# Thirteen held tables instead of ten, gathers in groups that wait for the landing of the group in front, and the second gram between the second and third layer

## The chip, the cores and the metric

One core of one Trainium2 chip. The metric is the device time of one execution in microseconds: 511.42 us, the median of three runs of the kernel before (511.13 to 512.32). Lower is better.

## The reference

2048 samples. For each, 26 rows of 128 floats are looked up, one in each of 26 tables; 13 tables have 1000 rows, the others 1250 to 125000. With the dense row that makes 27 feature vectors. All products of two different vectors (351), then the dense row, enter an MLP of 512, 256 and 1 outputs.

```
e = jnp.stack([tbl_0[ids[:, 0]], ..., tbl_25[ids[:, 25]]], axis=1)
combined = jnp.concatenate([dense[:, None, :], e], axis=1)
z = jnp.einsum('bfd,bgd->bfg', combined, combined)[:, iu, ju]
h = jnp.concatenate([z, dense], axis=1)
h = jnp.maximum(h @ W_top1 + b_top1, 0.0)
h = jnp.maximum(h @ W_top2 + b_top2, 0.0)
y = h @ W_top3
```

## The kernel before

The batch is done in eight turns (`s`) of 256 samples, each turn in two tiles (`t`) of 128. Turn 0 and VectorE's last turn are written out; the others are hardware loops on TensorE, ScalarE and VectorE, while SyncE and GpSimd are unrolled.

**Held tables.** `NUM_HOT` of the tables with 1000 rows stay in SBUF, split in a high and a low part (`hot_hi`, `hot_lo`). In turn 0 ScalarE rounds each (`round_hot`) and VectorE subtracts (`rest`, L264). A lookup of 256 samples is a product with a one-hot mask: VectorE makes the mask by comparing the ids, broadcast to all partitions, with row numbers (`compare`, L277), and TensorE multiplies (`hot`, L458), 8 matmuls with the high and 8 with the low part. `SLOTS` mask buffers are used in turn: the mask of feature f waits until feature f − SLOTS is multiplied (`hot_done`).

**Gathered tables.** The others are fetched by GpSimd, one indirect DMA per table and tile (L252), 64 KB each, into `rows`, in `GROUPS` of up to four features (feature 0 is the dense row, loaded by SyncE). TensorE transposes a group (`transposes`, L472), and ScalarE copies it to `feats`. `rows` holds one tile, so the gathers of a group of the next tile wait for the transposes of this one (`wait_rows_free`).

**Gram.** For each sample, TensorE multiplies 26 × 26 features (`grams`, L483, 128 products a tile, each two matmul records). ScalarE copies the first half of the samples, VectorE the second (`copy_gram`, L260), into `gram`, and nine DMAs of SyncE per tile move `gram` into `pairs` (`move_pairs`, L176), with the pairs on partitions. `pairs` is split in `pairs_hi` (ScalarE, `round_pairs`) and `pairs_lo` (VectorE, L286). Before the moves SyncE waits in `wait_gram`.

**MLP.** Layer 1 (`layer1a`, `layer1b`, L496 to L498) is three matmuls per chunk, in halves of two output blocks; layer 2 is L540 and layer 3 L548. Their ReLUs are on ScalarE (L378). The MLP of turn s − 1 is done within turn s.

**The order** within a turn is one list, `STEPS`, which TensorE and ScalarE both follow: tile 0's units (held pairs of tables and gathered groups mixed, `TILE0`), layer 1a, gram 0, then tile 1's groups mixed with layers 1b and 2, layer 3, gram 1. VectorE's order stands in its `turn`, SyncE's and GpSimd's in their loops. Units take three PSUM banks in turn. The outer loop of GpSimd:

```
for s in range(TURNS):
    for t in range(2):
        for g, features in enumerate(GROUPS):
            wait_rows_free(pool, s, t, g)
            for f in features:
                if f > 0:
                    pool.indirect_dma_start(...).then_inc(gathered[t][g], 16)
```

## Time and profile before

| | us |
|---|---|
| median of three runs | 511.42 |
| the profiled execution | 512.17 |
| its span, first to last instruction | 510.4 |
| TensorE busy (matmul) | 360.0 (71%) |
| VectorE busy | 242.9 (48%) |
| ScalarE busy | 153.6 (30%) |
| GpSimd busy | 254.2 (50%) |
| granted TensorE clock, mean | 0.839 |
| HBM read, whole span | 29.97 MB, 59 GB/s with the writes |

Busy time is a mean over stages. "Issue" is time in which an engine waited for nothing that the profile shows; "remote", or "another core or an unknown queue", is a wait whose releaser the profile cannot name (this kernel has one core). A matmul's end is modelled, its start is recorded. Gathers are the records of GpSimd; a record ends when the descriptors are made, and the data land later.

### The profile page before, as it was taken

The page shows a single profiled execution, that of the slowest core. Times are in us where ns is not written, and L with a number is a line of the kernel's source. Part 1 is how long each engine was busy: PE and PEld are TensorE (multiplying, and loading weights), DVE is VectorE, ACT ScalarE, POOL GpSimd, SP SyncE. Part 2 cuts the span into 40 slices and gives each one's busy share as a digit, 9 for nine tenths or more (in the row PEclk, how much of TensorE's full clock was granted, in tenths as well). Part 3 has the DMA queues.
Part 4 walks back from the last instruction along what each step waited for, and adds up shares of the span by engine and source line. Part 5 has one row for each costly group of instructions (what it writes and reads, how often), then busy time and mean ns, then how long its engine had stood idle before and what let it go on. Part 6 is the DMA issues. An engine that isn't in the chain of part 4 may idle for free.

```text
span 510.4 us, 13987 instructions
## 1 busy us (share of the span) xinstructions
PE 360.0 (71%) x6224; PEld 332.2 (65%) x6224; DVE 242.9 (48%) x172; ACT 153.6 (30%) x269; POOL 254.2 (50%) x260
## 2 busy tenths in 40 slices
PE   7695516977279763989369782897459882798927
PEld 6583406966179762989259781896439881797826
DVE  4995703827048270745429370673509451380220
ACT  2462401234122331324132241233232341223512
POOL 5887560655506474265635755264734745165000
PEclk9988656999569995899759986898959986698978
DMA  7992230211202131121303112131312112111000
GB/s 198 251 278 54 55 90 7 79 43 51 78 17 80 36 87 46 34 65 39 94 26 77 46 45 79 29 74 31 102 31 66 47 41 84 26 54 41 16 15 1
DMA packets 23322, 33.32 MB, mean 65 GB/s; under 512 B 6565, under 2 KB 15397, under 8 KB 23303
## 3 DMA queue, kind: packets, MB, share of 16 engines
q0 software_dynamic: 8192, 16.79, 12.6%
q1 hardware_dynamic: 14926, 16.20, 11.8%
q8 instruction: 12, 0.20, 0.2%
q10 hardware_dynamic: 186, 0.09, 0.1%
q14 instruction: 6, 0.05, 0.0%
HBM read 29.97 MB, written 0.01 MB: 59 GB/s over the span
## 4 chain that ended last, share of the span: by engine, by line
PE 56%; issue 18%; another core or an unknown queue 14%; ACT 7%; DMA 3%; SPq 2%; DVE 1%; ACTq 0%; DVEq 0%
PE psum L458 31%; PE psum L483 11%; PE psum L472 3%; DMA lows<-table 3%; ACT feats L336 3%; PE psum L548 3%; PE psum L496 2%; PE psum L497 2%; PE psum L498 2%; ACT gram L336 2%; PE psum L540 1%; ACT h L378 1%; SPq L208 1%; ACT dense_hi L336 1%
## 5 line engine op out<-in xcount | busy, mean ns | idle before, releaser
L252 POOL DMA_INDIRECT rows<-table,idx x256 | 254.0, 992 | 215.0 <-PE psum L472 114.2
L277 DVE TENSOR_TENSOR onehot<-ids_b,psum 125x2048 fp32r<-125x2048 int16 x80 | 180.2, 2283 | 18.5 <-PE psum L458 12.3
L260 DVE COPY gram<-psum 26x416 f32<-26x416 f32 x64 | 37.4, 584 | 182.6 <-PE psum L483 181.1
L336 ACT ACTIVATE feats<-psum 128x512 f32<-128x512 f32 (+1 forms) x120 | 77.4, 689 | 148.1 <-PE psum L458 106.9
L458 PE MATMUL psum<-onehot,hot_hi 125*128 125x256 f32 x640 | 99.2, 299 | 11.1 <-issue 6.8
L483 PE MATMUL psum<-feats 128*26 128x26 f32 x4096 | 64.3, 211 | 59.6 <-issue 55.7
L483 PEld LDWEIGHTS psum<-feats 128*26 128x26 f32 x4096 | 55.9, 125 | 70.8 <-issue 64.8
L458 PE MATMUL psum<-onehot,hot_lo 125*128 125x256 f32 x640 | 95.6, 291 | 4.4 <-issue 4.3
L458 PEld LDWEIGHTS psum<-onehot,hot_hi 125*128 125x128 f32 x640 | 86.5, 200 | 14.2 <-issue 9.0
L458 PEld LDWEIGHTS psum<-onehot,hot_lo 125*128 125x128 f32 x640 | 86.7, 198 | 6.3 <-issue 5.6
L336 ACT ACTIVATE gram<-psum 26x416 f32<-26x416 f32 (+1 forms) x72 | 35.5, 494 | 73.1 <-PE psum L483 54.5
L548 PE MATMUL psum<-h,w_sb 128*1 128x256 f32 x32 | 13.2, 560 | 60.2 <-ACT h L378 60.2
L378 ACT ACTIVATE h<-psum,b_sb 128x256 f32<-128x256 f32 x44 | 18.4, 470 | 102.2 <-remote 78.4
L548 PEld LDWEIGHTS psum<-h,w_sb 128*1 128x1 f32 x32 | 2.5, 99 | 66.4 <-ACT h L378 62.2
L472 PE MATMUL psum<-ident_sb,rows 128*128 128x128 f32 x272 | 42.0, 282 | 0.0
L496 PE MATMUL psum<-pairs_hi,w_hi 126*128 126x256 f32 (+1 forms) x96 | 28.5, 297 | 9.0 <-DVE pairs_lo L286 9.0
L472 PEld LDWEIGHTS psum<-ident_sb,rows 128*128 128x128 f32 x272 | 32.9, 145 | 1.2
L540 PE MATMUL psum<-h,w_sb 128*128 128x256 f32 x128 | 29.0, 379 | 0.0
L286 DVE TENSOR_TENSOR pairs_lo<-pairs,pairs_hi 126x768 fp32r<-126x768 f32 x8 | 7.9, 987 | 43.3 <-ACT pairs_hi L336 34.3
L497 PE MATMUL psum<-pairs_lo,w_hi 126*128 126x256 f32 (+1 forms) x96 | 28.2, 294 | 0.0
L498 PE MATMUL psum<-pairs_hi,w_lo 126*128 126x256 f32 (+1 forms) x96 | 28.1, 293 | 0.0
L540 PEld LDWEIGHTS psum<-h,w_sb 128*128 128x128 f32 x128 | 23.7, 190 | 2.9
(26 smaller groups left out, 167.7 us busy)
## 6 DMA issues: line engine op xcount, KB each, us to landing
lows<-table SPq DMA_DIRECT2D x10, 448.0 KB
rows<-table,idx POOLq DMA_INDIRECT x256, 2.5
ids_b<-hot_ids SPq DMA_DIRECT2D x8, 384.0 KB
ids_b<-hot_ids SPq DMA_DIRECT2D x8, 256.0 KB
rows<-dense SPq DMA_DIRECT2D x16, 64.0 KB
lows<-w SPq DMA_DIRECT2D x1, 1024.0 KB
pairs<-gram SPq DMA_DIRECT2D x16, 39.0 KB
lows<-table SPq DMA_DIRECT2D x10, 52.0 KB
```

The costliest lines, as they stand in the source:

```text
L252: pool.indirect_dma_start(out=rows[:, f, :], out_offset=None, in_=tables[f - 1], in_offset=bass.IndirectOffsetOnAxis(ap=idx[:, 2 * s + t, ...
L260: return nc.vector.tensor_copy(o, x)
L277: nc.vector.tensor_tensor(onehot[f % SLOTS][0:HP_ROWS, :, :], ids_b[0:HP_ROWS, f:f + 1, :].to_broadcast([HP_ROWS, HC, SB]), psum[0:HP_ROWS ...
L336: return nc.scalar.activation(o, x, ACT.Copy)
L458: mm = nc.tensor.matmul(psum[:, bank, (f % 2) * SB:(f % 2 + 1) * SB], part[0:HP_ROWS, f, c, :], onehot[f % SLOTS][0:HP_ROWS, c, :], start= ...
L472: mm = nc.tensor.transpose(psum[:, bank, m * P:(m + 1) * P], rows[:, f, :], ident_sb[:, :])
L483: mm = nc.tensor.matmul(psum[32 * q:32 * q + NJ, GP[h], k * NJ:(k + 1) * NJ], feats[:, t, n, 0:NJ], feats[:, t, n, 1:NF], start=True, stop ...
L496: nc.tensor.matmul(o, w_hi, x_hi, start=(n == 0), stop=False)
L497: nc.tensor.matmul(o, w_hi, x_lo, start=False, stop=False)
L498: return nc.tensor.matmul(o, w_lo, x_hi, start=False, stop=(n == ZC))
L540: mm = nc.tensor.matmul(psum[:, HP[0], m * SB:(m + 1) * SB], w2_sb[:, c, m * P:(m + 1) * P], h1[:, c, :], start=(c == 0), stop=(c == C1 - 1))
L548: mm = nc.tensor.matmul(psum[0:1, HP[1], 0:SB], w3_sb[:, m:m + 1], h2[:, m, :], start=(m == 0), stop=(m == C2 - 1))
```

## The change

- `NUM_HOT` goes from 10 to 13: the gathered tables go from 16 to 13, the groups from five (3, 4, 4, 4 and 1 gathers) to four (3, 4, 4 and 2), the held pairs from five to seven (the last has one table).
- `SLOTS` goes from 4 to 3. VectorE makes three masks ahead, and the `compare` in front of the second `copy_gram` is gone. `AHEAD` (4) keeps the rounding of tables in turn 0 as it was. The first part of the ids, loaded in two DMAs, is now three features, the second ten.
- `TILE0` has a new order. Layer 2 stands behind all of tile 1's transposes, gram 1 behind layer 2, layer 3 behind gram 1.
- GpSimd's `wait_landed`: a group's first gather waits until the group in front has landed, across tiles and turns. The third group of tile 0 also waits until the second gram of the turn before is done.
- `pairs_lo` is the memory of `pairs`, read as the other type: VectorE's subtraction overwrites `pairs`. So SyncE's moves of tile 0 wait for layer 1b of the turn before (`mlp_b`) instead of the split.
- The 32 transposes at the start are gone.

```diff
-NUM_HOT = 10
+NUM_HOT = 13
...
-    WARM = 32
...
-    SLOTS = 4
+    SLOTS = 3
+    AHEAD = 4
...
-    TILE0 = [("hot", 0), ("rows", 0, 0), ("hot", 1), ("rows", 0, 1), ("hot", 2), ("rows", 0, 2), ("hot", 3),
-             ("rows", 0, 3), ("hot", 4), ("rows", 0, 4)]
+    TILE0 = [("hot", 0), ("hot", 1), ("rows", 0, 0), ("hot", 2), ("rows", 0, 1), ("rows", 0, 2), ("hot", 3),
+             ("rows", 0, 3), ("hot", 4), ("hot", 5), ("hot", 6)]
...
-             + [("layer", "1b")] + TILE1[1:2] + [("dense",)] + TILE1[2:3] + [("layer", "2")] + TILE1[3:]
-             + [("layer", "3"), ("gram", 1)])
+             + [("layer", "1b")] + TILE1[1:3] + [("dense",)] + TILE1[3:] + [("layer", "2"), ("gram", 1), ("layer", "3")])
...
         pairs = sb("pairs", [P, ZC, SB])
+        pairs_lo = pairs[:, :, :].bitcast(fp32r)
         pairs_hi = sb("pairs_hi", [P, ZC, SB], fp32r)
-        pairs_lo = sb("pairs_lo", [P, ZC, SB], fp32r)
...
             def wait_gram(s, t):
                 if s == 0 and t == 0:
                     sp.wait_ge(zeroed, 1)
-                elif s > 0:
-                    sp.wait_ge(pairs_split, s)
+                elif t == 0:
+
+                    sp.wait_ge(mlp_b, 2 * s - 1)
...
         def _(pool):
+            def wait_landed(s, t, g):
+
+                if g > 0:
+                    t0, g0, s0 = t, g - 1, s
+                else:
+                    t0, g0, s0 = 1 - t, NG - 1, s - (t == 0)
+                if s0 >= 0:
+                    pool.wait_ge(gathered[t0][g0], 16 * sum(f > 0 for f in GROUPS[g0]) * (s0 + 1))
+
...
                         wait_rows_free(pool, s, t, g)
+                        wait_landed(s, t, g)
+                        if s > 0 and t == 0 and g == 2:
+
+                            pool.wait_ge(gram_done[1], 2 * s)
...
                 rest_of_dense(s)
-                if not last:
-                    compare(s + 1, 3, False)
                 copy_gram(dve, copy, 1, s, 1, first)
...
-                            for f in (2 * n[0] + SLOTS, 2 * n[0] + SLOTS + 1):
+                            for f in (2 * n[0] + AHEAD, 2 * n[0] + AHEAD + 1):
...
-            for f in range(SLOTS):
+            for f in range(AHEAD):
                 round_hot(f)
...
-                wait_feats(pe, s, "rows", t, NG - 1)
+                wait_feats(pe, s, *(TILE0, TILE1)[t][-1])
...
-
             pe.wait_ge(ident_in, 16)
-            for n in range(WARM):
-                nc.tensor.transpose(psum[:, HP[0], 0:P], ident_sb[:, :], ident_sb[:, :])
```

TensorE in the loop body, from tile 1's third group to the end of the turn. Before (L472 transposes, L540 layer 2, L548 layer 3, L483 gram):

```order
L472 MATMUL psum<-ident_sb,rows 128x128 [waits feats_out,gathered1_2]
...
L540 MATMUL psum<-h1,w2_sb 128x256 [waits relu_out]
...
L540 MATMUL psum<-h1,w2_sb 128x256 x4
L447 REGISTER_ALU [waits gathered1_3]
L472 MATMUL psum<-ident_sb,rows 128x128 [waits feats_out]
...
L447 REGISTER_ALU [waits gathered1_4]
L472 MATMUL psum<-ident_sb,rows 128x128 [waits feats_out]
L546 REGISTER_ALU
L548 MATMUL psum<-h1,w3_sb 1x256 [waits relu_out]
...
L483 MATMUL psum<-feats 26x26 [waits gram_out0]
```

The same piece now (L484 transposes, L552 layer 2, L495 gram, L560 layer 3):

```order
L484 MATMUL psum<-ident_sb,rows 128x128 [waits feats_out,gathered1_2]
...
L459 REGISTER_ALU [waits gathered1_3]
L484 MATMUL psum<-ident_sb,rows 128x128 [waits feats_out]
...
L552 MATMUL psum<-h,w_sb 128x256 [waits relu_out]
...
L552 MATMUL psum<-h,w_sb 128x256 x4
...
L495 MATMUL psum<-feats 26x26 [waits gram_out0]
...
L495 MATMUL psum<-feats 26x26 [waits gram_out1]
...
L560 MATMUL psum<-h,w_sb 1x256 [waits relu_out]
```

The transposes have moved in front of layer 2, and the gram stands between layer 2 and layer 3.

GpSimd's gathers from the start, before:

```order
L252 DMA rows<-table,idx 128x128 [waits idx_in]
L252 DMA rows<-table,idx 128x128 x15
L252 DMA rows<-table,idx 128x128 [waits rows_done]
L252 DMA rows<-table,idx 128x128 x2
L252 DMA rows<-table,idx 128x128 [waits rows_done]
L252 DMA rows<-table,idx 128x128 x3
```

And now, the second turn's groups 1 to 3 of tile 0:

```order
L266 DMA rows<-table,idx 128x128 [waits gathered0_0,rows_done]
L266 DMA rows<-table,idx 128x128 x3
L266 DMA rows<-table,idx 128x128 [waits gram_done1,gathered0_1,rows_done]
L266 DMA rows<-table,idx 128x128 x3
L266 DMA rows<-table,idx 128x128 [waits gathered0_2,rows_done]
L266 DMA rows<-table,idx 128x128
```

Every group has gained a wait for `gathered` of the group in front, and one group in eight a wait for `gram_done1`.

## Rows read from the trace of the kernel before

**Rows 1.** The page, the chain that ended last, by engine
```profile
PE 56%; issue 18%; another core or an unknown queue 14%; ACT 7%; DMA 3%; SPq 2%; DVE 1%; ACTq 0%; DVEq 0%
```

**Rows 2.** Windows: us, busy PE, PEld, DVE, ACT, POOL (instructions), clock, DMA share, GB/s
```profile
83.50:146.50 63.00, 44.14 (x774) 40.50 (x774) 28.82 (x21) 17.48 (x32) 30.48 (x32) 0.83 0.20 54
...
265.30:323.95 58.65, 42.46 (x775) 39.64 (x775) 28.61 (x21) 17.57 (x33) 31.24 (x32) 0.85 0.22 56
...
440.60:510.40 69.80, 54.87 (x842) 50.78 (x842) 22.84 (x21) 21.52 (x41) 15.09 (x16) 0.88 0.10 24
```

**Rows 3.** TensorE in turn 4: start, us, instructions [idle before, releaser]
```profile
284.44 1.12 PE L458 MATMUL psum<-onehot,hot_hi 125*128 125x256 f32 x8
285.40 1.12 PE L458 MATMUL psum<-onehot,hot_lo 125*128 125x256 f32 x8
...
290.57 0.44 PE L483 MATMUL psum<-feats 128*26 128x26 f32 x10 [1.06 <-issue]
...
293.63 2.95 PE L483 MATMUL psum<-feats 128*26 128x26 f32 x241 [1.19 <-issue]
296.52 0.65 PE L472 MATMUL psum<-ident_sb,rows 128*128 128x128 f32 x4
...
300.76 3.62 PE L540 MATMUL psum<-h,w_sb 128*128 128x256 f32 x16
304.22 0.71 PE L472 MATMUL psum<-ident_sb,rows 128*128 128x128 f32 x5
314.77 1.44 PE L548 MATMUL psum<-h,w_sb 128*1 128x256 f32 x3 [9.84 <-ACT h L378]
```

**Rows 4.** GpSimd in turn 4, its gathers
```profile
291.40 0.94 POOL L252 DMA_INDIRECT rows<-table,idx  x1 [0.30 <-issue]
297.44 0.94 POOL L252 DMA_INDIRECT rows<-table,idx  x1 [5.10 <-PE psum L472]
...
310.25 0.95 POOL L252 DMA_INDIRECT rows<-table,idx  x1 [0.30 <-issue]
314.18 0.94 POOL L252 DMA_INDIRECT rows<-table,idx  x1 [2.98 <-remote]
```

**Rows 5.** ScalarE in turn 4, the ReLUs of layers 1a and 2
```profile
293.79 0.84 ACT L378 ACTIVATE h<-psum,b_sb 128x256 f32<-128x256 f32 x2 [3.35 <-remote]
...
313.88 0.84 ACT L378 ACTIVATE h<-psum,b_sb 128x256 f32<-128x256 f32 x2 [9.68 <-remote]
```

**Rows 6.** TensorE in turn 7, layer 3 and the second gram
```profile
481.50 1.02 PE L548 MATMUL psum<-h,w_sb 128*1 128x256 f32 x4 [0.38 <-ACT h L378]
482.43 2.56 PE L483 MATMUL psum<-feats 128*26 128x26 f32 x256
```

**Rows 7.** The gathers' line, its duration and time from issue to landing
```profile
L252 POOL DMA_INDIRECT rows<-table,idx x256: 938/944/2111, 3.6 to 468.4; - x128
...
DMA to landing us min/median/max: 2.5/2.5/4.4
```

**Rows 8.** VectorE in turn 0, the masks of the last two tables
```profile
34.51 2.29 DVE L277 TENSOR_TENSOR onehot<-ids_b,psum 125x2048 fp32r<-125x2048 int16 x1
...
37.84 2.29 DVE L277 TENSOR_TENSOR onehot<-ids_b,psum 125x2048 fp32r<-125x2048 int16 x1
```

**Rows 9.** Turn 0: TensorE's grams, and GpSimd's first and last gather between them
```profile
45.47 0.57 PE L483 MATMUL psum<-feats 128*26 128x26 f32 x45 [2.82 <-ACT feats L336]
...
55.68 0.94 POOL L252 DMA_INDIRECT rows<-table,idx  x1 [3.69 <-PE psum L472]
...
58.98 0.55 PE L483 MATMUL psum<-feats 128*26 128x26 f32 x42 [1.12 <-ACT feats L336]
...
74.41 0.94 POOL L252 DMA_INDIRECT rows<-table,idx  x1 [0.30 <-issue]
...
78.71 2.34 PE L483 MATMUL psum<-feats 128*26 128x26 f32 x179 [0.50 <-issue]
```

**Rows 10.** SyncE in turn 4, the transfers of a tile's pairs
```profile
299.18 7.24 SPq L176 DMA_DIRECT2D pairs<-gram  x9
```

More of the change, by code:

```diff
@@ L43, in dlrm_tower @@
     HOT = [list(range(f, min(f + 2, NH))) for f in range(0, NH, 2)]
-    assert NG == 5 and len(HOT) == 5 and C1 == 4 and C2 == 2
-    TILE0 = [("hot", 0), ("rows", 0, 0), ("hot", 1), ("rows", 0, 1), ("hot", 2), ("rows", 0, 2), ("hot", 3),
-             ("rows", 0, 3), ("hot", 4), ("rows", 0, 4)]
+    assert NG == 4 and len(HOT) == 7 and C1 == 4 and C2 == 2
+    TILE0 = [("hot", 0), ("hot", 1), ("rows", 0, 0), ("hot", 2), ("rows", 0, 1), ("rows", 0, 2), ("hot", 3),
+             ("rows", 0, 3), ("hot", 4), ("hot", 5), ("hot", 6)]
     TILE1 = [("rows", 1, g) for g in range(NG)]
```

## The prediction

> **What bounds the kernel now.** I read the chain of waits first, then the turns by windows, then one turn engine by engine, then the first and the last turn.
>
> The chain [rows 1] is TensorE for 56%. It also holds 18% "issue" and 14% released by nobody the profile knows. So VectorE (48% busy) isn't the bound, and neither is the bandwidth. The turns [rows 2] show the shape: the kernel runs eight. From 83.5 to 440.6 us six equal ones take 357.1 us, 59.5 each, with TensorE busy for 42 to 44. Some 16 us of each turn are TensorE standing still.
>
> Where they stand is in turn 4, TensorE [rows 3]. From 265.3 to 286.5 it works without a gap on the held tables. After layer 1a the first gram begins at 290.57 and issues 10 matmuls. It then drips, and its other 241 come in one piece of 2.95 us at 293.63. Layer 2 and the last transposes end by 304.9. Layer 3 begins at 314.77, after 9.84 us of waiting for ScalarE. The second gram drips again and ends near 323.9.
>
> ScalarE [rows 5] waited for layer 2's signal until 313.88, although the last layer 2 matmul was over by 304.4. GpSimd [rows 4] issues a gather per 1.25 us (0.95 and 0.30 idle) without a pause from 297.44 to 311.2 and goes on at 314.18. At the first gram it is the same: the last gather ends at 292.34, the gram flows at 293.63, and layer 1a's signal reaches ScalarE at 293.79, over 4 us after its end. The control is turn 7 [rows 6], where no gathers are left: layer 3 waits 0.38 us, and all 256 matmuls of a gram take 2.56. The worst case is turn 0 [rows 9]: the second gram begins at 58.98, and 179 of its matmuls come in a piece at 78.71, after a run of gathers up to 75.35. **Reading:** while gathers run back to back, TensorE's completion signals come late, and tiny matmuls soon stop; both clear about 1.5 to 3 us after the last gather. That is inferred from coincidence, five places of one trace.
>
> The Trainium skill says the opposite (SBUF — State Buffer, "SBUF: two separate sides"): engine ports and DMA ports are disjoint, and a DMA and a compute operation cannot slow each other. By it the pauses buy nothing; that is the second rival below. Rows 3 to 6 speak against it here.
>
> **The change, part by part.**
>
> *More held tables.* Three tables move from gathers to one-hot matmuls. One table is 16 matmuls per turn, two pieces of 0.96 us [rows 3]: 1.91 us. Three are 5.7, less three transposes of 0.1: the table phase goes from 21.3 to 26.7 us on TensorE. VectorE must make 13 masks per turn at 2.29 us [rows 8]. Only three are made ahead now (onehot has three buffers, not four), so ten follow inside the phase: 22.9, behind the first feature (1.9) and perhaps 1 us of late signal, and ahead of the last feature (1.9): 27.7. VectorE passes TensorE by a little. I take 28.0. VectorE's whole turn, 13 masks (29.8) and the 5.7 that turn 4's 28.6 hold besides ten masks [rows 2], is 35.5 and doesn't bound.
>
> *Fewer and paced gathers.* 26 per turn instead of 32, in eight groups. A gather takes 2.5 us from issue to landing, 4.4 at most [rows 7]. With 1.25 us from gather to gather [rows 4] a pause costs 2.5 − 1.25, and some 0.2 for the wait: 1.5 us. GpSimd then needs 26 × 1.25 + 8 × 1.5 = 44.5 us per turn, under the turn I arrive at, so not a bound. At 4.4 us to landing it would be 57.7.
>
> *First gram.* Groups 2 and 3 of the first tile start once gram 1 is done, a little before the table phase, and land some 10 us into it. Tile 1's thirteen gathers and four pauses follow: 16.3 + 6 = 22.3, landed at 32.3. Gram 0 could start at 28.0 + 3.0 for layer 1a, so it drips for 1.3 us and ends at 35.3. Layer 1a is 286.5 to 289.5, where the 1.06 us of idle time before the gram's first piece begin [rows 3]; with the gram it was 9.9 us to 296.5, now 7.3.
>
> *Middle.* First transposes, layer 1b, transposes, layer 2: 296.5 to 304.9, 8.4 us; three transposes fewer, 8.1.
>
> *Second gram before layer 3.* Today 304.9 to 323.95, 19.05 us. Only groups 0 and 1 of the next first tile may now run before the gram is done: 3 × 1.25 + 1.5 and 4 × 1.25 + 1.5, 11.8 us from the first transposes at 35.5, so landed at 47.3. The gram stands ready at 43.4, drips, and ends at 47.3 + 2.6 = 49.9; ScalarE's ReLU of layer 2 is hidden under it; layer 3 adds 1.2, between the 1.0 and 1.4 of its records [rows 3, 6]: 51.1. This part is 7.7. Bounds: 4 from turn 7 [rows 6], where nothing drips, and 19 if nothing is cured.
>
> *Pairs in place.* pairs_lo now overwrites pairs, so the transfers of tile 0's pairs wait for layer 1b, 3.5 us behind gram 0, instead of a split long past. SyncE issues nine in 7.2 us [rows 10] and then the ids, for ten tables instead of six. They would start some 39 us into the turn, all be issued at 46, landed at 48.5. The copies of gram 1 want them at 49.9. Covered by 1.4 us; without that cover every late us delays VectorE's fourth mask.
>
> Sum of a turn: 28.0 + 7.3 + 8.1 + 7.7 = 51.1. Six turns: 306.6 against 357.1, **−50.5**.
>
> *Turn 0.* VectorE paces it: a mask and a split every 3.33 us [rows 8], three more, +10. The three more tables to load (1.5 MB) hide behind that pace. Gram 0 drips from 45.47 to 54.4 today [rows 9]; the gathers have landed before the later start, −5. Gram 1 took 24.4 us; now two groups and the gram, 14.4, −10. Together **−5**. The 32 transposes at the start vanish: at 1.2 instead of 2.4 GHz a feature takes at most twice its 1.91 us, 3.8, against a pace of 3.33, so 0.5 us each for a few features. I cost that at nothing, at most 2 us.
>
> *Turn 7.* Its table phase took 25.7 (a stall of 3 in it), now 28.0; a first gram perhaps 1.3 longer, layer 3 1.0 out of the way: **+2.6**.
>
> Total −52.9. The profiled execution took 512.17 us (span 510.4 and 1.8 around it); that gives 459.3. The median shown is 0.75 below it: **458.5 us**.
>
> **The rivals.**
>
> 1. *Gathers cost nothing any more.* If groups of at most four leave no backlog, both grams run as in turn 7: a turn is 27.5 + 6.3 + 8.1 + 4.0 = 45.9, six save 81.7 of 357.1 instead of 50.5, the time is 427. For: the table phases of turns 4 to 6 run beside groups of three and four gathers without a gap on TensorE; those of turns 1, 2 and 7 have a gap of 3 us, each beside eight gathers in a row. Against: a gram issues far faster than the tables' matmuls, and the one of turn 0 stopped 3.3 us after the gathers began anew, so within one group.
>
> 2. *The gathers were not the cause.* Then the late signal (9.9) and both drips stay: the turn is 28 + 9.8 + 8.1, 9.9 of waiting with half a gram under it, and 4.5 for the rest and layer 3: 60.3. Six turns cost 5, turn 0 10, turn 7 2: 528. Turn 7 and the instants of release speak against it. This is what the rule of the Trainium skill's SBUF page would do here.
>
> 3. *Late signals meet three mask buffers, and it is slower.* A buffer's round is a mask 2.29, a feature 1.91 and the signal's lateness L, over three buffers. At L = 1 the round is 1.7 per feature, hidden; from L = 2.7 it passes VectorE's 2.29. At 4.3, as after layer 1a [rows 3, 5], it is 2.83 per feature and the phase 36.8. With 23.1 for the rest a turn is 59.9, six cost 2, turn 0 saves 5 as before, turn 7 costs 11: 520. It decides from L = 4, a phase of 35.6. For: the lateness is seen. Against: the table phase at 284.44 runs on beside gathers, and TensorE waits for no mask there.
>
> 4. *Landing becomes the bound.* At 4.4 us to landing GpSimd needs 57.7 per turn: 6 × 57.7 = 346, the time is 498. Against: 4.4 is the worst, and the median 2.5 holds beside the pairs' transfers.
>
> The Trainium skill (DMA: Bandwidth & Descriptors, "Anatomy of one DMA") puts a gather's fixed cost at about 2.0 us, most of it the receipt of the write. By its figure, as an estimate, GpSimd needs 26 × 1.25 + 8 × 2.0 = 48.5 us per turn, still under the turn; the trace's median, 2.5 to landing, is of that size.
>
> **How the numbers follow.** My forecast, with its sizes off by up to 3 us per turn either way, has 0.72. Rival 1 has 0.13, rival 4 0.08, rival 2 0.03, rival 3 0.03, and 0.01 is for a wash. Three us on six turns and 5 on the first give 436 to 481; reaching toward rivals 1 and 4, the range is 430 to 486. About 0.2% is what a measurement of this kernel tells from no change. Faster 0.93, same 0.01, slower 0.06.
>
> **What would show it.** GpSimd's gathers stand in groups of two to four, with pauses near 1.5 us that a landing ends. ScalarE's wait for layer 2 falls from 10 us to under 4. Second grams end within 3 us of group 1's landing. Turns last 49 to 54 us, turn 0 some 78 to its end, and VectorE is busy for about 300 us. I am wrong if the wait before layer 3 stays near 10, if the table phase shows gaps of TensorE for VectorE's masks (over 30 us), or if GpSimd never waits for anything but landings.

## The result, and the profile after

The changed kernel takes **483.8 us** (median of 4, 477.34 to 485.17) against 511.87 us for the kernel before (4 runs, 511.13 to 512.34): ratio 0.9411, 95% interval 0.9318 to 0.9503. It is faster, as forecast, but by 28 us and not by 53: inside the range of 430 to 486, near its upper end. The four runs spread by 1.6%, where the kernel before spreads by 0.2%. The profiled execution took 484.05 us. The lines here are the page's: the busy time of each engine, TensorE's granted clock in 40 slices, and the chain by engine.

```profile
span 482.2 us, 14732 instructions
...
PE 393.7 (82%) x6528; PEld 361.2 (75%) x6528; DVE 298.3 (62%) x199; ACT 159.8 (33%) x272; POOL 204.5 (42%) x212
...
PEclk9975975799889999899989998999979998999968
...
PE 70%; issue 11%; DMA 10%; POOL 4%; SPq 2%; DVE 1%; ACT 1%; POOLq 0%; ACTq 0%
```

TensorE is 70% of the chain where it was 56% [rows 1]. "Issue" fell from 18% to 11%, and the 14% whose releaser the profile can't name are gone. Three stretches, the second and third answering to [rows 2] (window, its length, busy time and instructions of PE, PEld, DVE, ACT and POOL, clock, DMA share, GB/s):

```profile
87.50:142.40 54.90, 49.17 (x823) 45.98 (x817) 36.14 (x25) 17.54 (x31) 24.91 (x27) 0.91 0.22 59
248.40:301.90 53.50, 48.05 (x817) 43.13 (x816) 35.68 (x25) 17.92 (x32) 25.52 (x27) 0.97 0.20 57
408.90:482.20 73.30, 60.09 (x885) 54.87 (x884) 30.79 (x24) 22.00 (x41) 17.79 (x19) 0.93 0.10 26
```

Turns 1 to 6 begin at 87.5, 142.4, 196.1, 248.4, 301.9 and 356.0, turn 7 at 408.9: six in 321.4 us, 53.6 each, where 51.1 was predicted. Turn 0 ends at 87.5 (predicted 78.5), and what follows 408.9 lasts 73.3 (predicted 72.4). TensorE in turn 4, after the table phase of 248.4 to 276.3 (start, length, instruction, count, idle before it and what ended it):

```profile
279.26 0.67 PE L495 MATMUL psum<-feats 128*26 128x26 f32 x40
280.39 2.05 PE L495 MATMUL psum<-feats 128*26 128x26 f32 x216 [0.46 <-issue]
282.40 0.65 PE L484 MATMUL psum<-ident_sb,rows 128*128 128x128 f32 x4
...
290.62 0.52 PE L495 MATMUL psum<-feats 128*26 128x26 f32 x39
291.99 2.03 PE L495 MATMUL psum<-feats 128*26 128x26 f32 x145 [0.86 <-issue]
294.48 0.25 PE L495 MATMUL psum<-feats 128*26 128x26 f32 x5 [0.47 <-issue]
...
298.83 0.18 PE L495 MATMUL psum<-feats 128*26 128x26 f32 x1 [0.45 <-issue]
299.55 0.76 PE L495 MATMUL psum<-feats 128*26 128x26 f32 x45 [0.53 <-issue]
...
300.48 1.49 PE L560 MATMUL psum<-h,w_sb 128*1 128x256 f32 x3
```

The first gram flows almost at once (before: 10 matmuls, then a drip [rows 3]). The second begins at 290.62, flows for 184 matmuls, drips from 294.48 to 299, and ends in a piece of 45. Layer 3 follows without a wait. Turn 4 is shown because the kernel before was read there, and it isn't typical: of the six turns it has the shortest first gram and the longest second one. In turn 2 the second gram drips at its start instead, and is done sooner:

```profile
188.19 0.50 PE L495 MATMUL psum<-feats 128*26 128x26 f32 x36
...
192.08 2.38 PE L495 MATMUL psum<-feats 128*26 128x26 f32 x214 [0.53 <-issue]
```

In turn 4 ScalarE's ReLU of layer 2 waits 1.88 us instead of 9.68 [rows 5]:

```profile
290.72 0.84 ACT L390 ACTIVATE h<-psum,b_sb 128x256 f32<-128x256 f32 x2 [1.88 <-issue]
```

GpSimd's gathers in the same turn, the first of a group each but for 297.61, which is the last of its group (the idle time in brackets is the pause; within a group it is 0.30):

```profile
248.31 0.94 POOL L266 DMA_INDIRECT rows<-table,idx  x1 [4.45 <-DMA rows<-table,idx]
...
267.68 0.94 POOL L266 DMA_INDIRECT rows<-table,idx  x1 [2.32 <-DMA rows<-table,idx]
...
274.68 1.26 POOL L266 DMA_INDIRECT rows<-table,idx  x1 [2.31 <-DMA rows<-table,idx]
...
293.87 0.94 POOL L266 DMA_INDIRECT rows<-table,idx  x1 [2.99 <-DMA rows<-table,idx]
...
297.61 0.95 POOL L266 DMA_INDIRECT rows<-table,idx  x1 [0.31 <-issue]
301.14 0.94 POOL L266 DMA_INDIRECT rows<-table,idx  x1 [2.59 <-PE psum L495]
```

The gram flows again 1.0 us after the last gather has ended (297.61 + 0.95, then 299.55), and the gram's end releases the next gather at 301.14. From 248.31 to 301.14 are 52.8 us for 26 gathers and eight pauses, as long as the turn. It isn't GpSimd's time alone: three of the eight pauses end by TensorE, two by its transposes and one by the gram. In four of the six turns the wait for the gram is 4.5 to 4.8 us long, as here in turn 2, up to 2.5 longer than the shortest wait for a landing (2.3):

```profile
195.28 0.94 POOL L266 DMA_INDIRECT rows<-table,idx  x1 [4.79 <-PE psum L495]
```

So the two engines wait for each other by turns. Turn 0, first GpSimd and then TensorE:

```profile
14.12 1.79 POOL L266 DMA_INDIRECT rows<-table,idx  x1 [7.10 <-DMA rows<-table,idx]
...
27.82 0.94 POOL L266 DMA_INDIRECT rows<-table,idx  x1 [7.33 <-DMA rows<-table,idx]
...
40.97 0.94 POOL L266 DMA_INDIRECT rows<-table,idx  x1 [7.67 <-DMA rows<-table,idx]
```

```profile
40.75 1.11 PE L484 MATMUL psum<-ident_sb,rows 128*128 128x128 f32 x4 [9.90 <-DMA rows<-table,idx]
```

A group's pause is over 7 us there, beside the load of the held tables, and TensorE waits 9.90 us for rows.

### The profile page after: what moved, and what is told of

Its sections match the earlier page's. It is cut to its first block, busy times and chain, and to the rows that moved or that the text cites. A ratio compares the mean times of both kernels' runs of the same rounds, so it can differ in the third digit from the quotient of the medians.

```text
span 482.2 us, 14732 instructions
## 1 busy us (share of the span) xinstructions
PE 393.7 (82%) x6528; PEld 361.2 (75%) x6528; DVE 298.3 (62%) x199; ACT 159.8 (33%) x272; POOL 204.5 (42%) x212
## 3 DMA queue, kind: packets, MB, share of 16 engines
q0 software_dynamic: 6656, 13.64, 10.8%
## 4 chain that ended last, share of the span: by engine, by line
PE 70%; issue 11%; DMA 10%; POOL 4%; SPq 2%; DVE 1%; ACT 1%; POOLq 0%; ACTq 0%
PE psum L470 37%; PE psum L495 11%; DMA rows<-table,idx 8%; PE psum L552 5%; PE psum L484 5%; POOL rows L266 4%; PE psum L508 4%; PE psum L509 3%; PE psum L510 3%; SPq L176 2%; PE psum L560 2%; DMA pairs<-gram 1%; DVE gram L274 0%; DVE onehot L291 0%; DMA idx<-ids 0%
## 5 line engine op out<-in xcount | busy, mean ns | idle before, releaser
L266 POOL DMA_INDIRECT rows<-table,idx x208 | 204.3, 982 | 238.8 <-DMA rows<-table,idx 125.6
L291 DVE TENSOR_TENSOR onehot<-ids_b,psum 125x2048 fp32r<-125x2048 int16 x104 | 232.1, 2283 | 35.2 <-PE psum L470 25.2
L470 PE MATMUL psum<-onehot,hot_hi 125*128 125x256 f32 x832 | 125.8, 295 | 16.2 <-ACT hot_hi L348 10.6
L470 PEld LDWEIGHTS psum<-onehot,hot_hi 125*128 125x128 f32 x832 | 110.4, 197 | 25.9 <-issue 18.6
L470 PE MATMUL psum<-onehot,hot_lo 125*128 125x256 f32 x832 | 118.4, 286 | 0.0
L470 PEld LDWEIGHTS psum<-onehot,hot_lo 125*128 125x128 f32 x832 | 108.6, 194 | 0.6
L495 PE MATMUL psum<-feats 128*26 128x26 f32 x4096 | 61.8, 202 | 45.0 <-issue 43.5
L495 PEld LDWEIGHTS psum<-feats 128*26 128x26 f32 x4096 | 51.3, 115 | 57.5 <-issue 54.0
L484 PE MATMUL psum<-ident_sb,rows 128*128 128x128 f32 x224 | 34.2, 287 | 16.2 <-DMA rows<-table,idx 16.2
L484 PEld LDWEIGHTS psum<-ident_sb,rows 128*128 128x128 f32 x224 | 26.5, 147 | 17.6 <-DMA rows<-table,idx 16.9
L390 ACT ACTIVATE h<-psum,b_sb 128x256 f32<-128x256 f32 x44 | 18.4, 470 | 47.2 <-PE psum L510 24.7
L509 PE MATMUL psum<-pairs,w_hi 126*128 126x256 f32 (+1 forms) x96 | 29.0, 302 | 0.0
L552 PE MATMUL psum<-h,w_sb 128*128 128x256 f32 x128 | 28.9, 379 | 0.0
L552 PEld LDWEIGHTS psum<-h,w_sb 128*128 128x128 f32 x128 | 23.6, 190 | 2.9
L508 PEld LDWEIGHTS psum<-pairs_hi,w_hi 126*128 126x128 f32 (+1 forms) x96 | 20.3, 211 | 5.5 <-DVE pairs L300 5.5
L509 PEld LDWEIGHTS psum<-pairs,w_hi 126*128 126x128 f32 (+1 forms) x96 | 20.3, 212 | 0.0
L510 PEld LDWEIGHTS psum<-pairs_hi,w_lo 126*128 126x128 f32 (+1 forms) x96 | 20.1, 210 | 0.0
```

The costliest lines, as they stand in the source:

```text
L266: pool.indirect_dma_start(out=rows[:, f, :], out_offset=None, in_=tables[f - 1], in_offset=bass.IndirectOffsetOnAxis(ap=idx[:, 2 * s + t, ...
L291: nc.vector.tensor_tensor(onehot[f % SLOTS][0:HP_ROWS, :, :], ids_b[0:HP_ROWS, f:f + 1, :].to_broadcast([HP_ROWS, HC, SB]), psum[0:HP_ROWS ...
L390: nc.scalar.activation(dst[:, c, :], psum[:, bank, n * SB:(n + 1) * SB], ACT.Relu, bias=bias[:, c:c + 1]).then_inc(relu_out, 1)
L470: mm = nc.tensor.matmul(psum[:, bank, (f % 2) * SB:(f % 2 + 1) * SB], part[0:HP_ROWS, f, c, :], onehot[f % SLOTS][0:HP_ROWS, c, :], start= ...
L484: mm = nc.tensor.transpose(psum[:, bank, m * P:(m + 1) * P], rows[:, f, :], ident_sb[:, :])
L495: mm = nc.tensor.matmul(psum[32 * q:32 * q + NJ, GP[h], k * NJ:(k + 1) * NJ], feats[:, t, n, 0:NJ], feats[:, t, n, 1:NF], start=True, stop ...
```

## The experiments

Each kernel ran with the kernel before beside it. Kernels 1 to 8 (the first two sets) ran on one chip, where the kernel before took 511.63 and 513.67 us; the result's own runs, with 511.87, are counted with it. **Kernels 9 to 11 came onto a second chip of the same kind and kernel 12 onto a third, where the kernel before took 384.17 and 384.06 us**, at a granted clock of 0.96 instead of 0.84. Times are compared only within a chip; kernel 12 stands beside the other three because the kernel before takes the same on both. Kernels 2, 3, 4, 9 and 12 leave out lookups, so they give times and no usable result. Diffs are cut where `...` stands.

| kernel | us | ratio to before, 95% | turn, us |
|---|---|---|---|
| **first chip** | | | |
| before | 511.6 / 513.7 | 1 | 59.5 |
| changed (the result above) | 483.8 | 0.941 [0.932, 0.950] | 53.6 |
| 1. no pauses, no gate | 556.75 | 1.086 [1.080, 1.093] | 65.5 |
| 2. no gathers after turn 0 | 421.1 (one run) | | 44.9 |
| 3. plain loads by GpSimd | 418.29 (one run) | | 46.1 |
| 4. plain loads by SyncE | 413.85 (one run) | | 45.5 |
| 5. pauses alone on the kernel before | 548.52 | 1.068 [1.060, 1.076] | 61.8 |
| 6. no gate | 487.44 | 0.952 [0.945, 0.959] | 54.7 |
| 7. free start | 471.73 | 0.919 [0.913, 0.926] | 53.7 |
| 8. gate one group earlier | 494.23 | 0.966 [0.958, 0.974] | 54.6 |
| **second chip** | | | |
| before | 384.17 | 1 | |
| 9. rows in order, no pauses, no gate | 427.36 | 1.113 [1.107, 1.119] | 47.7 |
| 10. free start, up to two groups | 414.91 | 1.079 [1.076, 1.083] | 46.2 |
| 11. free start, pauses at the grams | 423.76 | 1.103 [1.101, 1.106] | 47.3 |
| **third chip** | | | |
| before | 384.06 | 1 | |
| 12. changed, rows in order | 461.07 | 1.201 [1.192, 1.211] | 51.8 |

A turn is the mean of turns 1 to 6 of the one profiled execution, from the start of one table phase to the next.

**1. No pauses, no gate.** Does the gain come from pausing, or from tables and order?

```diff
-                        wait_landed(s, t, g)
-                        if s > 0 and t == 0 and g == 2:
-                            pool.wait_ge(gram_done[1], 2 * s)
```

> The changed kernel with thirteen held tables, without the wait for landings and without the wait for the second gram: gathers run back to back as rows come free. Theory A (back-to-back gathers hold up TensorE's signals and its small matmuls): runs of seven or more gathers return, and with them waits of 8 us and more after layer 2 and grams of over 8 us; 500 to 530 us. Rival B (the pauses buy nothing; the gain comes from three tables fewer to gather and from the order): 470 to 485 us.

Measured 556.75 us, beyond both ranges. The pauses and the gate are worth 73 us; thirteen tables and the new order without them are 45 us slower than the kernel before. TensorE, then GpSimd's first and last of 13 gathers in a row, then two groups of the waits of the whole run (engine, line, releaser: us in all, times, longest):

```profile
266.91 0.36 PE L491 MATMUL psum<-feats 128*26 128x26 f32 x18
268.49 0.23 PE L491 MATMUL psum<-feats 128*26 128x26 f32 x3 [1.23 <-issue]
...
278.59 2.81 PE L491 MATMUL psum<-feats 128*26 128x26 f32 x221 [1.13 <-issue]
```

```profile
259.84 0.95 POOL L262 DMA_INDIRECT rows<-table,idx  x1 [16.29 <-PE psum L480]
...
275.09 0.94 POOL L262 DMA_INDIRECT rows<-table,idx  x1 [0.30 <-issue]
```

```profile
ACT h L386 <- remote: 55.2, 5, 11.5
...
DVE onehot L287 <- remote: 43.0, 8, 6.3
```

The gram begins at 266.91, stops 0.4 us later, and issues one to three matmuls at a time until the gathers end at 276.03; the rest comes in one piece 2.6 us later. "Remote" is a signal without a sender that the profile knows: VectorE's masks wait 43 us for such ones, and the table phase takes 35.6 us instead of 28. That is part of rival 3, whose own figure for the phase was 36.8. But not each signal is late, as it assumed: VectorE waits 6.3 us for one, and at the same time the table matmuls, 256 columns wide, stop like the small ones. In the same turn, from the tenth gather since 226.53 on:

```profile
239.88 0.52 PE L466 MATMUL psum<-onehot,hot_hi 125*128 125x256 f32 x3
...
243.41 0.28 PE L466 MATMUL psum<-onehot,hot_hi 125*128 125x256 f32 x1 [1.12 <-issue]
...
247.93 2.07 PE L466 MATMUL psum<-onehot,hot_hi 125*128 125x256 f32 x8 [1.17 <-DVE onehot L287]
```

A table that takes 1.9 us elsewhere takes from 239.88 to 246.8. The mask for the next one ends the wait last, 1.17 us later; the two delays lie over each other. So the reading "tiny matmuls stop" was too narrow.

**2. No gathers after turn 0.**

```diff
-                            if f > 0:
+                            if f > 0 and s == 0:
...
```

The pauses, and TensorE's waits for rows, go after turn 0 too.

> The changed kernel, but tables are gathered in turn 0 alone; later turns use the rows that lie there, so seven eighths of the lookups of the thirteen gathered tables are left out. Theory A: grams of 2.6 to 3.1 us, no wait of over 1 us for layer 2's signal, turns of 46 us, 425 to 435 us in all. Rival C (the drip is TensorE's own, from a low clock or from its instruction stream): grams still drip and the turns stay over 51 us, 465 to 480.

421.1 us, 4 below theory A's range, with grams (2.3 us) and turns (44.9) a little below those it named. Rival C is out. So the gathers still cost the changed kernel 63 us on this chip, of which turns 1 to 6 hold 52 (6 × 8.7).

**3. Plain loads in place of the gathers.** GpSimd issues them, with no pause and no gate; each moves 128 consecutive rows. The page counts 6656 packets and 13.64 MB in GpSimd's queue in either kernel.

```diff
-                            if f > 0:
+                            if f > 0 and s > 0:
+                                pool.dma_start(rows[:, f, :], tables[f - 1][P * (s % 7):P * (s % 7) + P, :]).then_inc(gathered[t][g], 16)
+                            elif f > 0:
```

> As the kernel without pauses, but from turn 1 on each indirect gather is a plain load of 128 consecutive rows of the same table, issued by GpSimd: the lookups of turns 1 to 7 are left out, the number and size of the transfers is the same. If what holds up TensorE is GpSimd making descriptors, or packets landing in SBUF, the time is that of the kernel without pauses within 3%, with the same drips. If it is the indirection itself, it comes near the kernel without gathers (425 to 440).

418.29 us, below the figure of the second theory (425 to 440) and far from the first. The rows are GpSimd's, then TensorE's:

```profile
248.81 5.27 POOL L262 DMA_DIRECT2D rows<-table  x10 [1.71 <-PE psum L482]
```

```profile
252.56 3.43 PE L493 MATMUL psum<-feats 128*26 128x26 f32 x256
255.81 1.02 PE L558 MATMUL psum<-h,w_sb 128*1 128x256 f32 x4
```

Ten loads in a row, 0.53 us each, run until 254.1, into a gram of which all 256 matmuls come in one piece, with layer 3 right behind. The same bytes, in as many packets, from the same queue, into the same place hold up next to nothing (this gram takes 3.3 us instead of 2.3). Traffic into SBUF as such is not what delays TensorE on this chip; the indirect gather is, by its form, the reading of its indices, its longer time on GpSimd (0.94 us against 0.53), or its scattered rows.

**4. The same loads from SyncE.** Against kernel 3, with the matching waits on TensorE:

```diff
+            def load_rows(s, t):
+                for g, features in enumerate(GROUPS):
+                    wait_rows_free(sp, s, t, g)
+                    for f in features:
+                        if f > 0:
+                            sp.dma_start(rows[:, f, :], tables[f - 1][P * (s % 7):P * (s % 7) + P, :]).then_inc(
+                                plain_in[t][g], 16)
...
```

> The same plain loads, issued by SyncE instead of GpSimd, without pauses; the lookups of turns 1 to 7 are left out. Theory A1 (it is GpSimd's making of descriptors in software, not the traffic): grams of 2.6 to 3.1 us, turns of 46 to 48 us, 430 to 450 in all. Theory A2 (it is packets that land in SBUF): grams and signals as late as with GpSimd's loads, within 4% of that kernel.

413.85 us, 4.4 less: what it costs that GpSimd issues them is small (one run each). It lies below A1's range, and within A2's 4%, which says nothing now that neither kernel has late grams. SyncE's queue moves the same 11.9 MB in 26208 packets where GpSimd's took 5824, so many small packets don't hold up TensorE either: a gram still takes 2.3 us.

**5. Pauses alone, on the kernel before.** Ten tables, old order, four mask buffers.

```diff
...
                         wait_rows_free(pool, s, t, g)
+                        wait_landed(s, t, g)
```

> The kernel before with one part of the change alone: a group of gathers begins when the one in front has landed. Ten held tables, the old order and four mask buffers stay. Theory (gathers in a row hold up small matmuls and TensorE's signals, whatever the order): the waits of about 10 us ahead of layer 2 and the drip of the first gram go, two to four us a turn less for each; but 17 gathers per tile with pauses of 2 to 4 us fill more of GpSimd's time. 485 to 500 us. Rival (the gain of the pauses comes only with the new order, since the old one has other things to fill the late signals): 505 to 515 us. A third way: with 34 gathers a turn and the pauses GpSimd becomes the bound, 515 us or more.

548.52 us, 35 *slower* than before; the third way. A turn of it:

```profile
342.90:405.20 62.30, 48.00 (x774) 43.77 (x774) 28.51 (x21) 17.39 (x32) 30.61 (x32) 0.83 0.19 53
```

GpSimd has 32 gathers a turn (not the 34 of the expectation) and ten pauses of 2.3 to 3.2 us: 32 × 1.25 and 10 × 2.2 make 62, and the turn is 62.3. So pauses alone don't pay with this many gathers. The parts of the change do not add up: pauses alone +35, tables and order alone +45, together −28.

**6. No gate.**

```diff
-                        if s > 0 and t == 0 and g == 2:
-                            pool.wait_ge(gram_done[1], 2 * s)
```

> The changed kernel without the one extra wait of GpSimd on the second gram; the wait for landing stays. Theory (gathers beside a gram cost it time): the second gram of each turn gets more gathers beside it and takes 1 to 3 us more, 484 to 505 us. Rival (the pauses are enough, and the extra wait only costs GpSimd time, which is nearly full): 470 to 480 us.

487.44 us against 483.8. It lies in the theory's range, but with overlapping intervals (0.952 and 0.941): a gain of the gate of some 4 us is likely and not established. In the profiled execution the second gram and layer 3 take 10.5 us a turn instead of 8.9, as the theory has it, and the first gram 0.8 less.

**7. Free start.** In turn 0 the first tile's gathers wait for nothing.

```diff
-                        wait_landed(s, t, g)
+                        if s > 0 or t == 1:
+                            wait_landed(s, t, g)
```

> The changed kernel, where the gathers of the first tile of turn 0 wait for nothing. Theory (in turn 0 the gathers land late because each pause waits for packets that share the queues with the tables' load, 7 to 8 us a pause; TensorE waits 9.9 us for one): 8 to 9 us less, all of it in turn 0, about 475 us. Rival (gathers in a row hold up the table phase of turn 0 just as much): no gain, 480 to 486 us.

**471.73 us, 12 less than the change**, and turn 0 ends at 75.1 instead of 87.5, all of the difference; a turn is 53.7 as before. The theory's 8 to 9 us were too few. (How much of the 12.4 is the edit is known only roughly: kernels 6 and 8 start turn 0 like the changed one and end it at 86.0 and 80.3.) GpSimd still has two long pauses there, but TensorE waits only 0.3 us for rows in turn 0:

```profile
28.39 0.95 POOL L267 DMA_INDIRECT rows<-table,idx  x1 [7.18 <-DMA rows<-table,idx]
...
40.50 0.94 POOL L267 DMA_INDIRECT rows<-table,idx  x1 [8.67 <-DMA rows<-table,idx]
```

It is the best real version on the first chip.

**8. Gate one group earlier.**

```diff
-                        if s > 0 and t == 0 and g == 2:
+                        if s > 0 and t == 0 and g == 1:
```

> The changed kernel, where GpSimd's extra wait on the second gram stands one group earlier, so that no group of the next turn but the first is gathered beside it. Theory (the gram's 11 us instead of 7.7 are the gathers beside it): it takes 3 to 6 us less per turn, 450 to 465 us. Rival (GpSimd then has too little time left for its groups, and the wait moves to the transposes of the rows): 484 us or more.

494.23 us, 10 more: the rival, on the time. In the profiled execution, its fastest (488.78), the turns are 1.0 us longer. The theory was right about the part that it named: the second gram and layer 3 take 4.3 us instead of 8.9, nearly the 3.9 of the kernel without gathers. But the gathers held back there come later: layer 1a and the first gram take 11.9 instead of 8.7, the table phase 29.3 instead of 27.6, the middle 0.7 more. The gathers' cost is moved, not saved.

**9. Rows in order, no pauses, no gate** (kernel 1 with other indices).

```diff
-        "ids": by_tile(ids)[:, :, cold].transpose(1, 0, 2),
+        "ids": np.broadcast_to(np.arange(128, dtype=np.int32)[:, None, None],
+                               (128, batch // 128, len(cold))),
```

> The changed kernel without pauses and without the gate (556.75 us), where the same indirect gathers read the rows 0 to 127 of each table in order instead of the looked up ones (it leaves out the lookups of the thirteen or so tables that are not held). It tells apart what the plain loads of the same 13.64 MB left open (418.29 us without any pause). Theory A (the form of the gather itself holds up the signals: one descriptor for each of 128 indices that the gather has to read first): about as slow, 530 to 557 us. Theory B (rows scattered over HBM do it): 415 to 440 us.

427.36 us, inside range B, and yet it proves nothing of B: it ran on the second chip, where the kernel before takes 384. There a gram beside an unbroken row of gathers looks like this (TensorE, then two of GpSimd's gathers, which stand every 1.25 us from 249.61 to 261.12):

```profile
255.44 0.76 PE L491 MATMUL psum<-feats 128*26 128x26 f32 x66
256.55 4.98 PE L491 MATMUL psum<-feats 128*26 128x26 f32 x190 [0.35 <-issue]
261.38 1.02 PE L556 MATMUL psum<-h,w_sb 128*1 128x256 f32 x4
```

```profile
253.35 0.94 POOL L262 DMA_INDIRECT rows<-table,idx  x1 [0.30 <-issue]
...
259.87 0.94 POOL L262 DMA_INDIRECT rows<-table,idx  x1 [0.30 <-issue]
```

It slows to 26 ns a matmul in its second piece, where a gram with nothing beside it takes 9, but it flows after one stop of 0.35 us, and layer 3 starts at once. So gathers still cost a gram something here: this one takes 5.9 us instead of 2.4. Rows in order aren't the reason why it is so little: kernel 11 shows the same with looked up rows.

**10. Free start, up to two groups under way.** With looked up rows again; a group waits for the one two in front.

```diff
-                if g > 0:
-                    t0, g0, s0 = t, g - 1, s
-                else:
-                    t0, g0, s0 = 1 - t, NG - 1, s - (t == 0)
+                n = NG * (2 * s + t) + g - 2
+                s0, t0, g0 = n // (2 * NG), n // NG % 2, n % NG
```

> The changed kernel with the gathers of the first tile free (471.73 us), where a group waits for the landing of the group two in front of it instead of the one in front, so up to eight gathers are under way. Theory (what harms is how many gathers stand in a row, and GpSimd's 50 us a turn are no bound of the turn): between the unpaced 556.75 and 471.73, 480 to 510 us. Rival (GpSimd's pauses are by now what a turn waits for): 455 to 470 us.

414.91 us, a comparison across chips and so neither. A turn of it:

```profile
212.60:257.10 44.50, 44.18 (x817) 41.89 (x816) 34.87 (x24) 17.84 (x33) 24.80 (x26) 1.00 0.25 68
```

44.5 us with TensorE busy for 44.2 and a clock of 1.00: this is nearly the turn that the kernel without gathers had on the first chip (43.8 to 44.4 in its turns 2 to 6), here with real gathers. It is also 12.5 us faster than kernel 9, which never waits: there the second gram and layer 3 take 6.5 to 7.8 us in turns 2 to 6, here 4.7. Kernel 10 has the gate and up to two groups under way, kernel 9 neither, and other indices; which of these gains the 12 us was not tried.

**11. Free start, pauses only at the grams.** Four of a turn's eight groups pause.

```diff
-                        if s > 0 or t == 1:
+                        if (s > 0 and t == 0 and g < 2) or (t == 1 and g > 1):
```

> The changed kernel with the gathers of the first tile free (471.73 us), and pauses only ahead of the four groups of a turn that stand beside the small matmuls of the grams and transposes; the four that fall in the table phase follow one another without a pause. Theory (only matmuls of a few columns and the handing over between engines suffer): the table phase stays at 28 us and GpSimd gains 6 to 12 us a turn, 455 to 472 us. Rival (gathers in a row hold up the table phase too, whose masks wait for TensorE's signals): its 28 us become 31 or more, 485 to 520 us.

423.76 us, 9 more than kernel 10; the range was made for the first chip. A second gram, beside a group of four looked up gathers that start at 254.87:

```profile
256.13 3.11 PE L496 MATMUL psum<-feats 128*26 128x26 f32 x120
259.65 1.39 PE L496 MATMUL psum<-feats 128*26 128x26 f32 x136 [0.41 <-issue]
```

Beside such a group the changed kernel's gram on the first chip issued one to six matmuls at a time; here it goes on at 26 ns each. The second gram and layer 3 take 5.7 to 6.9 us in turns 2 to 6 instead of 4.7: the pauses put gathers off until they run beside the gram. So between kernels 10 and 11 more pausing costs time, and between kernels 9 and 10 some restraint gains it.

**12. The change whole, rows in order.** Kernel 9's edit of the indices, made to the changed kernel; pauses and gate in place.

> The changed kernel whole, pauses and gate in place, where the gathers read the rows 0 to 127 of each table in order (it leaves out the lookups of the tables that are not held). What it tells depends on the chip, which the time of the kernel before shows. Where that is about 512 us, as in the first two sets of runs: theory A (the form of the gather holds up the signals, wherever its rows lie) 478 to 490 us, theory B (rows scattered over memory do it) 420 to 445 us. Where it is about 384 us, as in the third set: nothing is held up there, so A and B give the same, and the pauses only cost time: 425 to 445 us, 10 to 16 per cent slower than the kernel before; if pausing costs nothing there, 412 to 424 us.

It fell on the third chip, where the kernel before takes 384: 461.07 us, beyond the range given, and 34 more than kernel 9, which differs in pauses and gate alone (and in the chip). The waits show where (GpSimd's for landings, TensorE's transposes for rows):

```profile
POOL rows L266 <- DMA rows<-table,idx: 124.7, 45, 7.4
...
PE psum L484 <- DMA rows<-table,idx: 38.4, 13, 9.2
```

TensorE now waits for rows that the paced GpSimd brings late: 51.8 us a turn against 47.7.

## Why the prediction was right in sign and 25 us off

Part by part, in its own steps. The parts of a turn in us, mean of turns 1 to 6 of one profiled execution each (of turns 2 to 6 where none is paused), from the starts of TensorE's records:

| part | forecast | changed (shortest, longest) | no gate | gate earlier | no pauses | no gathers |
|---|---|---|---|---|---|---|
| table phase | 28.0 | 27.6 (27.3, 28.0) | 27.9 | 29.3 | 35.6 | 27.0 |
| layer 1a, first gram | 7.3 | 8.7 (6.1, 9.8) | 7.8 | 11.9 | 5.3 | 5.3 |
| middle | 8.1 | 8.5 (8.0, 9.5) | 8.5 | 9.2 | 8.0 | 8.0 |
| second gram, layer 3 | 7.7 | 8.9 (7.7, 11.3) | 10.5 | 4.3 | 16.0 | 3.9 |
| turn | 51.1 | 53.6 | 54.7 | 54.6 | 64.9 | 44.2 |

- **Table phase 28.0:** 27.3 to 28.0. Right, also that three mask buffers would do once the signals are no longer late; experiment 1 shows 35.6 when they are. (TensorE's "21.3 to 26.7" doesn't add up: 5.6 more than 21.3 is 26.9. Nothing hangs on it.)
- **First gram 7.3, middle 8.1, second gram and layer 3 7.7:** too short by 1.4, 0.4 and 1.2. In turn 4 alone it looks otherwise, 6.1, 8.2 and 11.3.
- **A pause costs 1.5 us:** the mis-sized term of the turn. Against the usual 0.30 the pauses cost 2.0 at best and up to 4.2 beside other transfers. In turns 1 to 6 the 31 waits that a landing ended hold 82.1 us, 2.65 each, so 2.35 more than the usual. By that, as an estimate, GpSimd needs 26 × 1.25 + 8 × 2.35 = 51.3 us without ever waiting for TensorE, and not 44.5. The 6.6 us of slack I had left it are gone, and "not a bound" was wrong. I took the landing time's median where the wait is for the last of a group, and counted no other transfers beside it. Experiment 5 shows a turn that is GpSimd's round, and experiment 8 that GpSimd can't make up a later start.
- **How it surfaces:** the gathers land later than forecast, the grams drip until they do, the second gram's end opens the gate, and the gathers behind it hold up the next first gram. This closed round of two engines is argued from the rows and from the parts of kernels 6 and 8, not tried by itself. Six turns: 321.4 instead of 306.6, +14.8.
- **Turn 0 −5:** it became +4. The failed step is "the three more tables to load hide behind that pace". They do for the masks, but the gathers' landings were not set beside that load: the first tile's groups pause behind it, 7 us each, and TensorE waits 9.90 us for rows. Experiment 7 gives up to 12.4 us back. +9.0.
- **Turn 7 +2.6:** +3.5, so +0.9, a net of parts. The first gram is 2.1 us longer than before and not 1.3. **Pairs in place** has no cover here: ScalarE's copy of the second gram waits 3.01 us for the pairs' transfer (1.11 before) and starts 4.0 us behind the gram's start instead of 1.7. The middle and the end are each under a us shorter. In turn 4 a similar wait of 2.77 us lies under the drip; there the pairs have landed 45.9 us into the turn, sooner than the 48.5 forecast, but the copy of the gram's first half wants them sooner still.

```profile
456.85 2.50 ACT L348 ACTIVATE gram<-psum 26x416 f32<-26x416 f32 x5 [3.01 <-DMA pairs<-gram]
```

The three add to 24.7 us, which is 459.3 to 484.0, the profiled time.

That the waits of 10 us went and the time fell is the mechanism that was forecast. That the time still lies in the range is in part luck: the range left 27.5 us above the forecast, and 25 of them were used up. It was luck too that the result ran where the kernel before takes 512 us.

**The reading** that gathers in a row delay TensorE's signals and stop small matmuls was inferred from coincidence. On the first chip experiments 1 to 3 confirm it, with two refinements: plain loads of the same bytes do not, and wide matmuls stop too. The rule of the Trainium skill (SBUF — State Buffer, "SBUF: two separate sides"), that a DMA and a compute operation cannot slow each other, therefore holds nearly for the plain loads (a turn of 46.1 against 44.9 with no gathers) and not for the indirect ones (65.5). Which way the disturbance takes no run shows. Whether the gathers' form or their scattered rows do it stays open: experiment 9 was to tell, and ran where the effect is weak. **Rival 1** (427 us) is wrong: groups of at most four still leave grams that drip. Its time is about that of the kernel without gathers, 421.1. **Rival 2** (528) falls for the first chip. **Rival 3** is part of what happens without the pauses (experiment 1). **Rival 4** is half true: the landings fill GpSimd's round, at 51 to 53 us and not 57.7.

**What the prediction could not see** is that the effect belongs to the chip. On two others the kernel before takes 384 us, and every version with thirteen tables that ran there is slower than it by 8 to 20%. The change as it is with looked up rows did not run there; kernel 11 pauses less and kernel 12 as much, and both are slower than the kernel before, so I infer that it would be too. Where signals are hardly late, three more tables are 5.7 us of TensorE a turn, 46 in eight turns, more than the 31 us that kernel 10 loses. Gathers are not free there either (experiments 9 to 11), but little is left for pauses to gain. In what runs without gathers beside it the chips agree: a first gram of 2.3 us and a middle of 8.0 in kernels 2 and 3 on the first chip and in kernel 10 on the second. No trace of the kernel before was taken on the second or third chip, and what differs between the chips stays open.

## What to carry to other kernels

Before paying TensorE work or pauses to get around a disturbance, time the kernel on a second chip: here one change is worth −6% on one, and its near relatives +8 to +20% on two others. When an engine is throttled to spare another, add up its whole round with the longest pause that shows beside other transfers, not the median; a wait on what it itself holds up closes a loop, and its round becomes the turn. Read every turn before the parts of one are called typical: turn 4 alone would put the whole error into the second gram. Here, pausing while the pipeline fills cost about 12 us.

## What the runs showed of the hardware that was not expected

- On the first chip, indirect gathers back to back let a gram issue one to three matmuls per 0.7 to 2.2 us for some 10 us on end, and ScalarE waited up to 11.5 us for one signal. Table matmuls of 256 columns stopped in the same way, for 7 us in a turn. Plain loads with the same 6656 packets and 13.64 MB did neither.
- A plain load issued by GpSimd takes it 0.53 us and lands in 2.0; a gather takes 0.94 to 0.95, with 0.30 idle behind it.
- Three chips of one kind gave 512, 384 and 384 us for one program, a third apart, with granted clocks of 0.84, 0.96 and 0.96. On the second, gathers beside a gram slow it from 9 to 26 ns a matmul, with looked up rows and with rows in order, and hardly stop it. Kernel 10, whose TensorE hardly waits, is granted 1.00 in the turn shown; whether the clock or the waiting comes first was not tried.
